# A two-layer recurrent mixture on one core: two program blocks joined into one, with the second layer's first steps woven into the last down projection

## The reference

```python
x = L0_attn_x                                   # (2, 1024, 512)
xn = _layernorm(x)
s = down(keep_largest_half(silu(xn @ Wg.T)) * (xn @ Wu.T))      # inner width 1376
g = _silu(xn @ ternary(W).T + bias)
x = x + s * g                                   # first layer
xn = _layernorm(x)
h = xn @ Win.T + bin                            # width 64
for l in range(4):
    y = silu(layernorm(h) * w + b)
    h = h + scl * real(scan(y, p_l, last_l))    # complex decay p_l, over the sequence
    h = h + W2_l silu(W1_l layernorm(h) + b1_l) + b2_l
s = layernorm(h) @ Wout.T + bout
g = _silu(xn @ (W + low_rank).T + bias)
x = x + s * g                                   # second layer
```

## Time and profile before

| | |
|---|---|
| median of 3 runs | 626.37 us (625.25 to 627.36) |
| the profiled execution | 626.69 us, of which the profile's span is 624.9 us |
| mean granted clock of TensorE | 0.976 of full speed |
| busy: TensorE, VectorE, ScalarE, GpSimd | 592.0, 481.8, 340.3, 188.3 us |
| end of the first block's last down product | about 447.9 us |
| start of the second block on TensorE | 452.69 us |
| phase 1, first product | 479.39 us |

### The profile page before, as it was taken

How to read it: one execution, slowest core, us unless ns; L and a number is a source line. 1 busy time by engine, 2 the same in 40 slices (tenths; PEclk the granted TensorE clock), 3 DMA queues, 4 the chain that set the end, 5 groups by cost and what they waited for, 6 DMA issues and landing times. The chain is left out here.

```text
span 624.9 us, 8833 instructions
## 1 busy us (share of the span) xinstructions
PE 592.0 (95%) x2852; PEld 460.1 (74%) x2852; DVE 481.8 (77%) x940; ACT 340.3 (54%) x571; POOL 188.3 (30%) x308
## 2 busy tenths in 40 slices
PE   7989999999999999999999999999698999999775
PEld 6877887888888888888888888886575656656432
DVE  6998799897888788788878878768586666767556
ACT  6877386267438418725752861775463444455420
POOL 2332002001001000200100010189885666663344
PEclk9999999999999999999999999999989999999887
DMA  9911000200020030021003001091030000000015
GB/s 352 326 51 34 2 0 2 69 34 2 6 95 0 0 101 0 0 68 33 0 0 101 0 0 68 3 344 34 3 69 1 0 1 1 1 1 1 1 67 201
DMA packets 17194, 32.35 MB, mean 52 GB/s; under 512 B 3238, under 2 KB 3750, under 8 KB 17164
## 3 DMA queue, kind: packets, MB, share of 16 engines
q1 hardware_dynamic: 17164, 31.99, 14.8%
HBM read 24.63 MB, written 7.35 MB: 51 GB/s over the span
## 5 line engine op out<-in xcount | busy, mean ns | idle before, releaser
L877 DVE TENSOR_SCALAR_CACHE_REDUCE junk_d<-k_buf,cand 128x1376 int8<-128x1376 f32 x56 | 91.9, 1641 | 0.3
L669 ACT ACTIVATE junk_a<-k_buf,cand 128x1376 int8<-128x1376 f32 x56 | 80.6, 1439 | 0.6
L648 ACT ACTIVATE s_buf<-ps_a 128x1376 f32<-128x1376 f32 x16 | 21.1, 1321 | 95.2 <-PE ps_a L1187 91.2
L1220 PE MATMUL ps_a<-wd_hi,zt_hi 128*128 128x512 f32 (+1 forms) x176 | 71.9, 408 | 0.2 <-DVE zt_lo L996 0.2
L1220 PE MATMUL ps_a<-wd_hi,zt_lo 128*128 128x512 f32 (+1 forms) x176 | 69.2, 393 | 0.0
L1220 PE MATMUL ps_a<-wd_lo,zt_hi 128*128 128x512 f32 (+1 forms) x176 | 68.8, 391 | 0.0
L533 POOL TENSOR_TENSOR xres<-xres,gate 128x512 f32<-128x512 f32 x12 | 22.3, 1862 | 130.9 <-DVE gate L1003 130.9
L525 POOL TENSOR_TENSOR rstd<-var_eps,expo 128x2 f32<-128x2 f32 x7 | 4.9, 704 | 162.3 <-DVE var_eps L799 162.3
L1187 PE MATMUL ps_a<-wg_hi,xt_hi 128*128 128x512 f32 (+1 forms) x192 | 51.9, 379 | 0.8 <-ACT xt_hi L614 0.8
L1187 PE MATMUL ps_b<-wu_hi,xt_hi 128*128 128x512 f32 (+1 forms) x192 | 51.8, 378 | 0.0
L1187 PE MATMUL ps_a<-wg_lo,xt_hi 128*128 128x512 f32 (+1 forms) x192 | 50.7, 372 | 0.6 <-DVE wg_lo L782 0.6
(11 more groups left out here) (249 smaller groups left out, 1373.4 us busy)
## 6 DMA issues: line engine op xcount, KB each, us to landing
xres<-in_x SPq DMA_DIRECT2D x8, 512.0 KB, 3.3
out<-arena SPq DMA_DIRECT2D x16, 256.0 KB, 2.0
xin<-in_x SPq DMA_DIRECT2D x7, 512.0 KB, 4.1
x_scratch<-xres SPq DMA_DIRECT2D x6, 514.0 KB, 3.9
arena<-x_scratch SPq DMA_DIRECT2D x3, 1028.0 KB, 12.7
m_buf<-in_wg_t SPq DMA_DIRECT2D x2, 688.0 KB, 5.5
k_buf<-in_wg_t SPq DMA_DIRECT2D x2, 688.0 KB, 8.0
m_buf<-in_wu_t SPq DMA_DIRECT2D x2, 688.0 KB, 7.1
```

Source lines behind the costliest of these rows:

```text
L648: act.activation(s_buf[:, t, :], ps_a[:].rearrange("p a n -> p (a n)")[:, 0:INNER], ACT.Silu).then_inc(s_ready, 1)
L669: act.activation(junk_a[:], k_buf[:, 1, :], ACT.Sign, bias=c, scale=-1.0, accum_out=below[:, 1:2]).then_inc(act_step, 1)
L877: dve.tensor_scalar(junk_d[:], k_buf[:, 0, :], c, -float(DROP), ALU.is_lt, ALU.add, accum_out=e).then_inc(cnt_dve, 1)
L1220: last = pe.matmul(ps_a[:, t, :], zs, ws[0:rows, c, :], start=(c == 0 and n == 0), stop=(c == CHUNKS - 1 and n == 2))
```

## The change

There is one block. The second layer's code follows the first's on each engine; in place of the barrier there are waits on semaphores where memory is shared.

- **Memory.** Small constants and `fold` now lie over the gate weights, `x1` over the end of the up weights. Constants, parameters and tables can start when the last gate projection is done. A tile of `xt` lies over down weights, so its copy waits for a down group: tiles 0 to 3 for group 46, 4 to 7 for 47, the others for 48. `xt` holds tiles in the order in which they are taken.
- **TensorE.** Tiles 0 to 7 are transposed between the last three down groups, into banks free by then.
- **VectorE** copies tiles 1, 3 and 8 to 11, makes layer 0's six table products, and does the last down gate after them. The means of w2 move behind phase 0.
- **GpSimd** makes all powers first, then the sum of tile 14, the low rows, the sum of tile 15 and its root. It makes no table of layer 0.
- **SP.** The parameters' loads go out after the last gate projection, the bias rows' after the memset, w2 and b1 after the last mask, w1 and wout after the last transpose.
- The phases from 1 on are the same.

The diff is cut; indentation is dropped where whole functions only moved.

```diff
 def second_layer():
-    sp.wait_ge(up_done, TILES)
+    sp.wait_ge(gate_done, TILES)
     ...
+    sp.wait_ge(up_done, TILES)
     for i in range(3):
         load_x1_group(sp, ORDER[i])
 ...
+TOKEN_BANK = (0, 1, 2, 3, 4, 5, 0, 1, 4, 5, 0, 6, 4, 5, 0, 6)
+def token_bank(i):
+    return ([bank2[1]] + bankg + [bank2[0]] + bankx + [bank1[1]])[TOKEN_BANK[i]]
+def takes_on_vector(i):
+    return i in (1, 3) if i < PER_HALF else i < PER_HALF + 4
+def covered_until(i):
+    return LAST_DOWN - 2 if i < 4 else LAST_DOWN - 1 if i < 8 else LAST_DOWN
 ...
 # GpSimd
-pool.wait_ge(up_done, TILES)
+pool.wait_ge(gate_done, TILES)
 ...
-residual(PAIRS - 1, 0, resident=True)
 tables_powers(pool, 0, 0, 2)
+pool.wait_ge(up_done, TILES)
+residual(PAIRS - 1, 0, resident=True)
+tables_powers(pool, 0, 2, 4)
 residual(PAIRS - 1, 1, resident=True)
 norm2_root(pool, 1, 0, LOADED, expo[:])
-tables_powers(pool, 0, 2, FINE_BITS)
-tables_powers(pool, 1, 0, COARSE_BITS - 1)
-for t in range(2):
-    residual(PAIRS, t, resident=True)
+tables_powers(pool, 0, 4, FINE_BITS)
+pool.wait_ge(q_done, TILES)
+pool.memset(row_f[:], 0.0).then_inc(rows_zero, 1)
+tables_powers(pool, 1, 0, COARSE_BITS)
+residual(PAIRS, 0, resident=True)
+pool.wait_ge(x1_ready, TILES - 1)
+rows_low(32)
+pool.wait_ge(rows_lo, 2)
+rows_low(96)
+pool.wait_ge(rows_lo, 3)
+residual(PAIRS, 1, resident=True)
+norm2_root(pool, 2, LOADED, TILES, expo2[:, 0:TILES - LOADED])
+second_root(0, 0)
-pool.memset(row_f[:], 0.0).then_inc(rows_zero, 1)
-tables_powers(pool, 1, COARSE_BITS - 1, COARSE_BITS)
-norm2_root(pool, 2, LOADED, TILES, expo2[:, 0:TILES - LOADED])
-tables_some(0, 3)
-tables_some(3, 6)
-root(0, 0)
 ...
 # ScalarE, behind norm2_apply of tiles 8 to 11
+for k in range(2):
+    weights_high(k)
+zt_high(PAIRS, 5)
+take_tile(0)
+take_tile(2)
+for k in range(2, KH):
+    weights_high(k)
 ...
+for i in range(4, PER_HALF):
+    take_tile(i)
+for k in range(2):
+    gate_hi(k)
+squares(0, 0)
+for k in range(2, 4):
+    gate_hi(k)
+for m in range(LOADED, TILES):
+    norm2_apply(act, 2, m)
+norm_out(0, 0, ACT.Silu, pcol(0, C_L1W), pcol(0, C_L1B))
+for i in range(LOADED, TILES):
+    take_tile(i)
+gate(0)
 ...
 # VectorE, behind zt_low(8, 4) and down_gate(8, 0)
+weight_means(win, 0, KH, win_in, 16, win_s)
+take_means(win, 0, KH, win_s)
+take_tile(1)
+zt_low(PAIRS, 5)
+for k in range(2):
+    weights_low(k)
+take_tile(3)
+for k in range(2, KH):
+    weights_low(k)
+dve.wait_ge(bc_ps, 1)
+dve.tensor_copy(bias_c[:], bank2[0][:, 0:DEPTH + 1]).then_inc(bc_s, 1)
+tables(dve, dve_passed, 0, 0, 6)
+down_gate(PAIRS, 1)
+token_stats(0)
+h_in(0)
+token_stats(1)
+token_means()
+norm2_eps(dve, LOADED, TILES)
+take_tile(PER_HALF)
+variance(0, 0)
+norm2_negated(dve, 2, LOADED, TILES)
+for i in range(PER_HALF + 1, PER_HALF + 3):
+    take_tile(i)
+widen(0, 0)
+take_tile(PER_HALF + 3)
+normed(0, 0)
+decay(0, 0)
+gate_lo(0)
 ...
 # TensorE, behind zt_transpose(last, 4)
-down(last, 3)
-zt_transpose(last, 5)
-down(last, 4)
-down(last, 5)
+for i in range(2):
+    tokens(i)
+down(last, 3)
+zt_transpose(last, 5)
+for i in range(2, 4):
+    tokens(i)
+down(last, 4)
+for i in range(4, 6):
+    tokens(i)
+center_biases()
+for i in range(6, PER_HALF):
+    tokens(i)
+down(last, 5)
+project_in(0)
+for i in range(PER_HALF, PER_HALF + 4):
+    tokens(i)
+variances(0, 0)
+gates(2 * KH)
+spread(0, 0)
+for i in range(LOADED, LOADED + 2):
+    tokens(i)
+gates(KH + 1)
+for i in range(LOADED + 2, TILES):
+    tokens(i)
+gates(4)
+project_in(1)
+gates(9)
```

More of the change, by code:

```diff
@@ L148, in mixture_kernel @@
         u0 = over_weights(2, DEPTH)
+        rho = over_weights(DEPTH)
+        part = over_weights(2)
+        off = over_weights(KH + 2 * DEPTH)
+        bias_c = over_weights(DEPTH + 1)
+        carry = over_weights(2)
+        fold = over_weights(8, HID)
+        assert cursor[0] <= 2 * N_W
+        f_a, f_b, f_wt = fold[:, 0:2, :], fold[:, 2:4, :], fold[:, 4:8, :]
+        hs = [fold[:, 0:4, :], fold[:, 4:8, :]]
+        work = over_weights(4 * SEQ)
+        xn = work.rearrange("p (t n) -> p t n", n=HID)
+        w_re, w_im, u_re, u_im = (work[:, j * SEQ:(j + 1) * SEQ] for j in range(4))
+        sq = w_re
+        win = over_weights(KH, DIM)
+        stats2 = over_weights(2, 6)
+        rs2 = over_weights(TILES)
+        nmr = over_weights(TILES)
+        assert cursor[0] + TILES * ROW <= N_ARENA
+        x1 = over_weights(TILES, ROW)
         x1_in = [sem(f"x1_in{i}") for i in range(3)]
@@ L334, in mixture_kernel @@
             one = sb("one", [P, 1])
[L335 to L374, removed]
@@ new lines, in tables, with pick @@
+        def tables(engine, passed, l, first, last):
+            done = [N_SMALL + 6 * l + first]
+            def pick(j, fine):
+                v = small[:, j, l, 0:FINE if fine else COARSE]
+                v = v.rearrange("p (o n) -> p o n" if fine else "p (n o) -> p n o", o=1)
+                return v.to_broadcast([P, COARSE, FINE])
+            fr, fi, cr, ci = pick(0, True), pick(1, True), pick(2, False), pick(3, False)
+            co, si, t = (v.rearrange("p (a b) -> p a b", b=FINE)
+                         for v in (rot[:, l, 0, :], rot[:, l, 1, :], tbig[:]))
+            steps = ((t, ci, fi, ALU.mult), (co, cr, fr, ALU.mult), (co, co, t, ALU.subtract),
+                     (t, ci, fr, ALU.mult), (si, cr, fi, ALU.mult), (si, si, t, ALU.add))
+            for o, a, b, op in steps[first:last]:
+                engine.wait_ge(tb, done[0])
+                settled(engine, passed)
+                engine.tensor_tensor(o, a, b, op).then_inc(tb, 1)
+                done[0] += 1
@@ L1610, in _ @@
                     if feeds:
[L1611 removed]
+                        variance(n, d)
                     if l < DEPTH:
[L1613 to L1622 removed]
@@ L2097, in _program @@
+                else:
+                    pe.wait_ge(f_free, FF * DEPTH)
+                    output(4)
+                    output(5)
+                    variances(q, c)
+                    output(6)
+                    output(7)
+                    spread(q, c)
+                    pe.wait_ge(ln_o[c], q + 1)
+                    for m in range(PER_HALF, TILES):
+                        output(m)
 def _program(nc, args, out):
```

2862 lines of the change are left out of this document (1404 added, 1458 removed).

## The result

The changed kernel takes 622.19 us (median of 4 runs, 621.26 to 623.36) against 626.87 for the kernel before, measured beside it (median of 4): a ratio of 0.9938, 95% interval 0.9914 to 0.9962. It is faster by 0.6% by that ratio, by 4.7 us between the two medians, and not by the 1.4% of the forecast of 617.6; it lies 0.3 us above the upper end of the range, 621.9. The profiled execution is the longest of the four: 623.36 us, of which the span is 621.6, at a mean granted clock of 0.976 as before.

The account below looks back on a forecast made before the run. Dense TensorE work, split by a gap awaiting GpSimd's queue and then low clock, was taken as the bound. Variances at 472.7 against 482.13 give 9.4, taken as 9.0: 626.69 to 617.7, given as 617.6 us; range 613.9 to 621.9.

Parts of the forecast that it names:

- The gap: Between the two blocks TensorE idles 4.8 us, waiting for GpSimd's queue; the barrier alone costs 0.4 us.
- The gap stays: Rival: the pause between blocks is the fetch of new instructions, so it and its low clock remain; 625.4 us, chance 0.03.
- TensorE's queue: From 439.76 to phase 1's variances: 31.4 us of work without waits; with waits they start at 472.7, not 482.13.
- GpSimd's powers: 77 power instructions and a memset, started at 426.4, end at 445.1, 3.8 us before VectorE's tables ask for them.
- the rival in which they are late: VectorE's first table product waits for GpSimd's last power; at 0.48 us an instruction 632.1 us, slower; chance 0.04.
- ScalarE's copies: Token-tile copies and bias work on ScalarE end near 450.4, before the last down group ends, so they are hidden.
- VectorE's queue behind the moved tables: Six table products, 4.5 us in all, end at 453.4; VectorE is free 0.8 us before h arrives (the cover).
- Rows on GpSimd: Two 1x1024 subtractions at 2.3 us each, from 448.1 to 452.7, before the last sum can start at 454.1.
- The main case: Variances of phase 1 come 9.4 us earlier, gain taken as 9.0: 617.6 us (616 to 619.5), chance 0.60.
- one collision: Allowance that cut the gain from 9.4 to 9.0 us, for one VectorE-GpSimd port clash mostly hidden by the 0.8 cover.
- tables and GpSimd collide: Rival: VectorE's table products and GpSimd's rows take turns, 9.1 us, ending at 457.2; gain 5.3, 621.4 us, chance 0.2.
- The clock at the end: Rival: after 585 steps may fall in a high-clock stretch, about 3 us better, 614.7 us, chance 0.13.

Follow-up runs that it names:

- experiment 7: Kernel before the change, with one doubling of GpSimd's powers moved from the first block's end to the second's start: 626.79 us, ratio 1.0004.
- experiment 1: Changed kernel without GpSimd's two low-row subtractions (high part of each bias added twice, output wrong): 617.24 us against 627.12, ratio 0.984.
- experiments 4: Changed kernel with 30 idle transposes on TensorE, 18 before tile 11 and 12 before the first variances: 621.29 us, ratio 0.9908.
- experiment 5: Changed kernel, whole, with both low rows made early by one VectorE instruction over all partitions and ScalarE's row copy moved ahead: 615.32 us, ratio 0.9833.
- experiment 8: Changed kernel with jobs exchanged: six table products back on GpSimd, the two low rows on VectorE where the tables stood: 617.68 us, ratio 0.9856.
- experiment 9: Changed kernel with one of GpSimd's two low rows (partition 96, low part of the second bias) left out: 619.01 us, ratio 0.9871.

## Why the prediction was wrong

**The gap, right.** The end of the block waited for GpSimd's queue, the barrier itself cost 0.4: experiment 7 takes work out of that queue and the second block starts as much earlier as expected, and the changed kernel has no gap. "The gap stays" falls.

**TensorE's queue, right.** Without the rows the variances of phase 1 come at 471.93 where the sum said 472.7; that run began 1.1 us earlier in the first place, so the sum of products and waits, 32.9, was 0.3 short. The waits named in it were there: 0.6 for the spread (0.49 in experiment 1), 0.7 for xs_lo (0.76). Two small readings in it were off and changed nothing: the first eight transposes take 1.73 from start to start (1.94 is the row's length, and was set against 0.88 from start to start), and the carry takes 1.34 by the earlier trace rows, not 1.42.

**GpSimd's powers, right.** Forecast to be done at 445.1, they were at 445.7; the rival in which they are late falls. ScalarE's copies were hidden, as said.

**VectorE's queue behind the moved tables, nearly right as a sum.** The products took 0.69 each, but follow one another every 0.84, not 0.74: waiting for the one before costs 0.15. That is 0.4 in all (4.9 in experiment 1, where the sum had 4.5), and leaves a cover of 0.47 where it had 0.8.

**Rows on GpSimd: the step that failed.** The forecast read: "From 448.1 they end at 452.7, before the last sum can start (454.1)". They took 2.69 each (2.3 was entered, within the bounds of 1.15 and 4.1), and that they ended at 452.6 was luck in part, since they also began 1.0 earlier. Wrong was the question. I asked who on GpSimd waits behind the rows, found nobody, and entered nothing; the cost lay on the engine beside it. The main case had 0.4 us for "one collision". The two rows held VectorE for 4.2, of which 0.47 was covered, and behind that came 1.9 of low clock: 5.7 of distance (37.57 - 31.84), and a gain of 9.9 us (experiment 1: 627.12 - 617.24) cut to 4.7. The 0.95 beside the sum of tile 14 comes on top in VectorE's queue, in experiment 1 as well. In the profiled executions the account closes so: the variances come 4.1 earlier, the part behind them is 0.8 longer, and the execution is 3.3 shorter (626.69 - 623.36); the other 1.4 of the medians' 4.7 is the spread of executions.

**The rival "tables and GpSimd collide", right.** It had the mechanism, the place and the price nearly: 621.4 against 622.19. It had 9.1 us for the six tables taking turns with the rows; in fact the first row met a split of weights, and only the second a table. It lacked the low clock after TensorE's waits, though the earlier trace rows showed a clock of 0.55 after the gap, so that its number came so near is luck in part: it had phase 1 begin 5.3 earlier, and it began 4.1 earlier. It should have been the forecast. What I held against it, the many products that keep 0.69 beside GpSimd in the phases, is no evidence, and the trace of the kernel before could have told me. The long row of L1816 in the earlier trace rows was two hits, 1.04 and 1.77, and not one. The other fourteen splits of that line meet only GpSimd's root of 128x8, which holds no product (0.68 each). The products of the phases that meet a GpSimd instruction of 128x512 have an input in PSUM, or meet only its last 0.13 us, or started before it, as here, where GpSimd pays (1.51 instead of 1.07):

```profile
493.55 0.75 DVE L1794 SCALAR_TENSOR_TENSOR h<-arena,h 128x512 f32<-128x512 f32 x1
493.72 1.51 POOL L1564 TENSOR_TENSOR tbig<-arena 128x512 f32<-128x512 f32 x1 [1.55 <-DVE h L1775]
```

Where GpSimd started first, VectorE's product was held near the end of that program too, and so was a copy with one input, which takes 0.43 elsewhere:

```profile
600.19 1.27 POOL L1586 TENSOR_TENSOR arena<-xt,arena 128x512 f32<-128x512 f32 x1 [9.75 <-DVE xt L1811]
600.75 1.26 DVE L1806 TENSOR_TENSOR arena<-xt,arena 128x512 f32<-128x512 f32 x1
...
607.21 2.49 POOL L1586 TENSOR_TENSOR arena<-xt,arena 128x512 f32<-128x512 f32 x2
607.27 1.48 DVE L1735 COPY arena<-lnr 128x512 f32<-128x512 f32 x1
```

In the eleven traces of this study 46 products of 128x512 with both inputs in SBUF started after a GpSimd instruction of 128x512 or 1x1024 that was still at work for at least 0.15 us; each ended 0.54 to 0.56 after it. Another 99 started before one, and each kept its 0.68 to 0.75.

By the rule of the Trainium skill (GPSIMD Engine Reference, section 1, Specifications: GpSimd shares its SBUF interfaces with VectorE and contends with instructions of VectorE that read two SBUF inputs or run in a 2-port performance mode) that rival's time was the one to expect. The trace agrees for two inputs: 2.76 instead of 0.69 for a product that met a row of GpSimd's; the small copy from PSUM between the two took 0.15 as ever. Whether the held copy of one input ran in such a mode, no run here shows.

**The clock at the end, not there.** From phase 1's variances to the end of the span the changed kernel takes 143.55 us, the kernel before 142.77. The profiled runs of this study lie between 141.9 and 144.2 there. The two shortest, experiments 4 and 5 (141.9 and 142.1), have a first low stretch of about 7 us (the granted clock is 0.51 over 582.2 to 589.1 in experiment 5), where the changed kernel has one of about 10 (0.50 over 585.3 to 595.5). So the better end exists, worth some 1.5 us and not 3; which execution gets it, no run here explains, and the two groups in experiment 5 are of one and the same kernel.

## What to carry to other kernels

When work is moved to an engine "with nothing to do", look up not only who waits behind it on that engine, but what its neighbour runs in the same microseconds: an instruction of VectorE with both inputs in SBUF that starts while GpSimd works on a long one waits for the rest of it, so a one-partition row of 1024 elements on GpSimd (2.7 us) is dearer than the same on VectorE (1.2). Which of the two pays is decided by which starts first. A row in one partition is best joined with others into one instruction over all partitions: 1.28 us for both rows here. And removing a gap is worth only what the next engine in line allows: half of this one, by itself, gave nothing.

## What the runs showed that I had not expected

- The hold is mutual, and the instruction that starts second pays; GpSimd's, when it is first, takes some 0.2 longer (the sum of tile 14 takes 1.30 beside a split, that of tile 15 1.09). In experiment 8 GpSimd's product of 1.28 us took 2.04 beside VectorE's rows, and these took 1.91 and 2.20 instead of 1.22. In the kernel before, both rows of VectorE started 0.3 ahead of a table product and kept 1.22, and the two products took 1.84 and 2.07: the longest product in the earlier trace rows was such a one.
- GpSimd's side needs no two inputs: a row of one input (1.37 us) held VectorE's table product for 0.77. But its root of 128x8 (1.64 us) held no product of VectorE; whether the length in each partition or the operation decides that, no run shows.
- GpSimd took 2.69 us for a subtraction of 1x1024 and 1.37 for the same length with one input, where 128x512 takes 1.1 to 1.3 with two inputs and 0.69 with one (414.42 in the kernel before, 1.38 for two of them): twice the elements in each partition take twice as long, and one partition is no cheaper than 128. Each 2.69 began with about 0.4 us beside a product of VectorE already at work, so part of it can be a hold in the other direction; no run has this row alone.
- The clock falls by steps and not in proportion: TensorE waited 1.35 us before the variances both in the changed kernel and in experiment 9. With 1.93 us of waiting just before, the next six microseconds were granted 0.50; without, 1.00. In experiment 7 waits of 1.52 and 1.81 with 5.6 us of products between them left it at 1.00.
